# Last layer of a graph network: product order changed, from adj-first in split float32r to weights-first in plain float32, diagonal on VectorE

## What is computed

```
h = relu(layernorm(x))
h = relu(adj @ (h @ Wg0 + bg0)); h = relu(adj @ (h @ Wg1 + bg1))
for p in 1..4:                      # an LSTM over windows of p nodes, its last state
    h[:, p-1::p, :] = lstm_last(Wih[p-1], Whh[p-1], ..., windows of h)
x = x + h
h = relu(layernorm(x))
x = x + diag(adj) @ (h @ W[0]) + triu(adj, 1) @ (h @ W[1]) + tril(adj, -1) @ (h @ W[2]) + bias
```

## Time and profile before

| | |
|---|---|
| median of 3 runs | 424.93 us (424.89 to 425.09) |
| the profiled execution | 424.94 us |
| its span, first to last instruction | 423.2 us |
| granted TensorE clock | 1.00 |
| busy: TensorE / VectorE / ScalarE / GpSimd | 97% / 78% / 66% / 9% |
| first unit of group 1, 2, 3 begins | 110.04, 209.94, 311.48 us |

### The profile page before, as it was taken

One profiled execution on the slowest core, in us unless ns is written; L12 is line 12 of the kernel. 1 busy time (PEld: TensorE's weight loads), 2 busy tenths in 40 slices (PEclk: granted clock), 3 DMA queues, 4 the chain that ended last, 5 costly groups with the idle time before them and its releaser, 6 DMA issues.

```text
span 423.2 us, 7879 instructions
## 1 busy us (share of the span) xinstructions
PE 411.4 (97%) x2628; PEld 368.5 (87%) x2628; DVE 329.7 (78%) x849; ACT 280.8 (66%) x571; POOL 39.2 (9%) x46
## 2 busy tenths in 40 slices
PE   8999999999999999999989999999999999999897
PEld 7787889997878899999868889999887889999787
DVE  5669999989885788797967678878988777767841
ACT  4667766775966576766876576677596676667542
POOL 4910002001100002000200001100110000000300
PEclk9999999999999999999999999999999999999999
DMA  7900000000001000000001000000000000000011
GB/s 229 366 29 2 0 0 2 2 0 2 0 21 38 14 0 15 4 17 2 2 2 38 31 0 12 1 19 0 1 1 19 27 0 14 0 20 2 12 53 62
DMA packets 6081, 11.17 MB, mean 26 GB/s; under 512 B 1056, under 2 KB 4768, under 8 KB 5536
## 3 DMA queue, kind: packets, MB, share of 16 engines
q1 hardware_dynamic: 6048, 10.77, 7.2%
HBM read 6.57 MB, written 4.19 MB: 25 GB/s over the span
## 4 chain that ended last, share of the span: by engine, by line
PE 70%; DVE 19%; ACT 6%; issue 2%; DMA 1%; POOL 1%; SPq 0%; DVEq 0%; ACTq 0%
PE PS L490 9%; PE PS L481 9%; PE PS L482 9%; PE PS L550 9%; PE PS L509 5%; PE PS L533 5%; PE PS L506 5%; PE PS L505 5%; PE PS L430 3%; PE PS L422 3%; ACT GT L750 3%; PE PS L440 3%; PE PS L407 3%; ACT TC L759 2%; DVE CS L874 2%
## 5 line engine op out<-in xcount | busy, mean ns | idle before, releaser
L750 ACT ACTIVATE GT<-PS,BG 128x256 f32<-128x256 f32 (+2 forms) x312 | 158.5, 563 | 48.7 <-PE PS L509 25.9
L481 PE MATMUL PS<-HH,WIH 128*128 128x256 f32 (+2 forms) x312 | 108.3, 348 | 2.3 <-DVE HH L898 1.8
L482 PE MATMUL PS<-HH,WIL 128*128 128x256 f32 (+2 forms) x312 | 102.7, 330 | 0.0
L490 PE MATMUL PS<-HL,WIH 128*128 128x256 f32 (+2 forms) x294 | 97.4, 331 | 0.3
L759 ACT ACTIVATE TC<-CS 128x512 f32<-128x512 f32 (+2 forms) x88 | 45.1, 512 | 47.5 <-DVE CS L874 31.8
L481 PEld LDWEIGHTS PS<-HH,WIH 128*128 128x128 f32 x312 | 59.0, 189 | 7.2 <-DVE HH L898 2.8
L482 PEld LDWEIGHTS PS<-HH,WIL 128*128 128x128 f32 x312 | 59.0, 189 | 3.4
L490 PEld LDWEIGHTS PS<-HL,WIH 128*128 128x128 f32 x294 | 55.5, 189 | 6.0 <-DVE HL L913 1.7
L509 PE MATMUL PS<-SL,WHH 128*128 128x256 f32 (+2 forms) x192 | 60.1, 313 | 0.0
L351 POOL TENSOR_TENSOR RS<-VE,NHALF 128x8 f32<-128x8 f32 (+2 forms) x15 | 26.5, 1766 | 360.8 <-DVE VE L822 360.8
L505 PE MATMUL PS<-SH,WHH 128*128 128x256 f32 (+2 forms) x192 | 59.8, 312 | 0.0
(11 more groups left out here) (91 smaller groups left out, 596.2 us busy)
## 6 DMA issues: line engine op xcount, KB each, us to landing
X<-x_tbd SPq DMA_DIRECT2D x3, 1024.0 KB, 11.6
out_tbd<-X SPq DMA_DIRECT2D x15, 192.0 KB, 1.9
X<-x_tbd SPq DMA_DIRECT2D x4, 256.0 KB, 4.3
WI<-wih_t SPq DMA_DIRECT2D x1, 1024.0 KB, 5.6
out_tbd<-X SPq DMA_DIRECT2D x7, 128.0 KB, 1.7
WH<-whh_t SPq DMA_DIRECT2D x1, 768.0 KB, 7.1
out_tbd<-X SPq DMA_DIRECT2D x1, 256.0 KB, 2.0
WL<-w_l SPq DMA_DIRECT2D x1, 192.0 KB, 7.0
```

The lines of the kernel that those rows point to most:

```text
L481: pe.matmul(dst, WIH[:, p - 1, cols], x_high, start=True, stop=False)
L482: pe.matmul(dst, WIL[:, p - 1, cols], x_high, start=False, stop=False)
L490: mm = pe.matmul(dst, WIH[:, p - 1, cols], x_low, start=False, stop=(j == 0))
L750: act.activation(GT[:, s, q, 0:n], bank(s, q)[:, 0:n], ACT.Tanh if q == C else ACT.Sigmoid, bias=BG[:, 4 * (p - 1) + q:4 * (p - 1) + q + 1 ...
```

## The change

The product is turned round, and works by quads of 4 batches:

- **Centre.** VectorE subtracts the mean from four batches at once (`centre`, 512 columns). It replaces all normalising and splitting; the reciprocal root is applied later.
- **Turn.** Four transposes by TensorE (`last_turn`), then ScalarE's relu of 512 columns into SBUF (`turn_up`).
- **Value.** Per batch one plain float32 matmul of 384 columns against the three weights side by side (`last_value`); ScalarE's copy of it (`copy_value`) applies the reciprocal root and sorts the three parts. The values lie in the raw LSTM weights' buffers.
- **Sum.** Per quad a bias matmul and two plain float32 matmuls of 512 columns, with adj's upper and lower triangle (`last_sum`). The diagonal part is a multiply and add on VectorE (`add_own`), then `add_out` adds the sum.

The tables hold the new pieces with their bank (0 or 1) and what must be read first. `f_after` makes a unit's forget gate wait until the piece on its bank has been read. `early`, `mid` and `late` say where VectorE does its part in a unit: before the cell, after it, or after the low half.

```diff
+START = {(0, 2): (Piece(TURN, 0, 0, None),), (1, 1): (Piece(TURN, 1, 1, None),),
+         (1, 2): (Piece(VALUE, 0, 0, (TURN, 0)),), (2, 0): (Piece(VALUE, 1, 1, (TURN, 1)),),
+         (2, 2): (Piece(VALUE, 2, 0, (VALUE, 0)),), (3, 0): (Piece(VALUE, 3, 1, (VALUE, 1)),),
+         (3, 1): (Piece(VALUE, 4, 0, (VALUE, 2)),), (4, 0): (Piece(SUM, 0, 1, (VALUE, 3)),),
+         (4, 1): (Piece(VALUE, 5, 0, (VALUE, 4)),), (4, 2): (Piece(VALUE, 6, 1, (SUM, 0)),),
+         (5, 0): (Piece(VALUE, 7, 0, (VALUE, 5)),), (5, 1): (Piece(TURN, 2, 1, (VALUE, 6)),),
+         (6, 0): (Piece(VALUE, 8, 1, (TURN, 2)),), (6, 2): (Piece(VALUE, 9, 1, (VALUE, 8)),),
+         (6, 3): (Piece(VALUE, 10, 1, (VALUE, 9)),), (7, 3): (Piece(VALUE, 11, 0, (FORGET, 6)),)}
 STEADY = Plan(
+    at={**START, (5, 2): (Piece(SUM, 1, 0, (VALUE, 7)),),
+        (7, 4): (Piece(SUM, 2, 0, (VALUE, 11)),), (9, 0): (Piece(TURN, 3, 1, (FORGET, 7)),),
+        (10, 3): (Piece(VALUE, 12, 1, (TURN, 3)),), (11, 3): (Piece(VALUE, 13, 0, (FORGET, 10)),),
+        (12, 3): (Piece(VALUE, 14, 1, (FORGET, 11)),), (13, 3): (Piece(VALUE, 15, 0, (FORGET, 12)),),
+        (13, 4): (Piece(SUM, 3, 0, (VALUE, 15)),)},
+    f_after={6: (SUM, 1), 7: (VALUE, 10), 10: (SUM, 2), 11: (VALUE, 12), 12: (VALUE, 13), 13: (VALUE, 14), 16: (SUM, 3)},
+    early={4: ((ADD, 0),), 7: ((OWN, 2),), 13: ((OWN, 3),)},
+    mid={3: ((OWN, 0),)},
+    late={0: ((CENTRE, 2),), 1: ((CENTRE, 3),), 5: ((OWN, 1), (ADD, 1)), 7: ((ADD, 2),), 13: ((ADD, 3),)})
 LATE = Plan(
+    at={**START, (7, 4): (Piece(SUM, 1, 0, (VALUE, 11)),), (13, 4): (Piece(SUM, 2, 0, (FORGET, 12)),)},
+    f_after={6: (VALUE, 7), 7: (VALUE, 10), 10: (SUM, 1), 16: (SUM, 2)},
+    early={4: ((ADD, 0),), 7: ((OWN, 2),)},
+    late={0: ((CENTRE, 2),), 1: ((CENTRE, 3),), 5: ((OWN, 1),), 7: ((ADD, 1),), 13: ((ADD, 2),)})
...
+            def last_turn(g, q, ps):
+                pe.wait_ge(centred, QUADS * g + q + 1)
+                for n in range(PACK):
+                    mm = pe.transpose(as_batches(ps)[:, n, :], H3[:, q * PACK + n, :], IDENT[:, :])
+            def last_value(g, n, ps):
+                pe.matmul(ps[:, 0:PARTS * D], H3T[:, q % 2, b * T:b * T + T],
+                          WL1[:, :, :].rearrange("p k e -> p (k e)"), start=True, stop=True).then_inc(value_mm, 1)
+            def last_sum(g, q, ps):
+                pe.matmul(as_batches(ps), TWO[:, :], BIAS2[:, :].unsqueeze(1).broadcast_to([T, PACK, D]),
+                          start=True, stop=False)
+                pe.wait_ge(value_sb, G * g + q * PACK + PACK)
+                for k in range(SIDES):
+                    mm = pe.matmul(ps, ADJ2[:, k, :], values(q)[:, 1 + k, :], start=False, stop=(k == SIDES - 1))
...
+            def turn_up(g, q, ps):
+                act.activation(H3T[:, q % 2, :], ps, ACT.Relu).then_inc(turn_sb, 1)
+            def copy_value(g, n, ps):
+                act.activation(values(q)[:, 0:PARTS, b * D:b * D + D],
+                               ps[:, 0:PARTS * D].rearrange("p (k e) -> p k e", k=PARTS), ACT.Copy,
+                               scale=RS2[:, n:n + 1]).then_inc(value_sb, 1)
...
+            def centre(g, q):
+                dve.tensor_tensor(H3[:, quad(q), :], X[:, part, :],
+                                  MINUS2[:, quad(q)].unsqueeze(2).broadcast_to([T, PACK, D]),
+                                  ALU.add).then_inc(centred, 1)
+            def add_own(g, q):
+                dve.wait_ge(value_sb, G * g + q * PACK + PACK)
+                dve.scalar_tensor_tensor(out=X[:, part, :], in0=as_batches(values(q)[:, 0, :]), scalar=DIAG[:, 0:1],
+                                         in1=X[:, part, :], op0=ALU.mult, op1=ALU.add).then_inc(own_ready, 1)
+            def add_out(g, q, ps):
+                dve.wait_ge(out_mm, QUADS * g + q + 1)
+                dve.tensor_tensor(X[:, part, :], as_batches(ps), X[:, part, :], ALU.add).then_inc(out_ready, 1)
...
             def next_graph(i):
...
                 bias_y(1, i + 1)
+                centre(i, 0)
+                centre(i, 1)
                 stats2(1, i)
                 low_h(0, i + 1)
```

More of the change, by code:

```diff
@@ L66 @@
 WARM = 16
-ADJP, OUTP = "adj", "out"
+TURN, VALUE, SUM, FORGET = "turn", "value", "sum", "forget"
+Piece = namedtuple("Piece", ["what", "n", "s", "after"])
 Plan = namedtuple("Plan", [
     "at",
[L75 to L79, removed]
+    "f_after",
+    "quads",
+    "early",
+    "mid",
+    "late",
 ])
 FILL = {4: 6, 9: 6, 15: 5}
[L86 to L92, removed]
@@ L106 @@
-CHUNKS = len(STEADY.chunks)
-TAIL = range(LATE.chunks[-1][0], G)
-NORM_AT, SPLIT_AT = 0, 2
+OWN, ADD, CENTRE = "own", "add", "centre"
+START = {(0, 2): (Piece(TURN, 0, 0, None),), (1, 1): (Piece(TURN, 1, 1, None),),
[6 more added lines that the diff above has]
+         (6, 3): (Piece(VALUE, 10, 1, (VALUE, 9)),), (7, 3): (Piece(VALUE, 11, 0, (FORGET, 6)),)}
@@ L117 @@
+LATE_LOW_AT = {7: ("wi",), 9: ("wh",), 18: ("bias",)}
 LATE_ROW_AT = 20
-LATE_ORDER = ("wi", "wh", "adj", "bias")
+LATE_ORDER = ("wi", "wh", "bias")
 CELL_EARLY = (1, 2, 15)
-def chunk_of(plan, n):
-    c = next(c for c, (first, size) in enumerate(plan.chunks) if first <= n < first + size)
-    return c, n == plan.chunks[c][0], n == sum(plan.chunks[c]) - 1
 LN_STATS_AT = {4 + k: range(3 * k, min(3 * k + 3, G)) for k in range(6)}
@@ L320, in _, with store @@
                 sp.dma_start(X[:, g * G:(g + 1) * G, :], x_tbd[:, g * G:(g + 1) * G, :]).then_inc(x_rest, 16)
[L323 to L326, removed]
+            def store(i):
+                for q in range(QUADS):
+                    sp.wait_ge(out_ready, QUADS * i + q + 1)
+                    part = bass.ds(i * G + q * PACK, PACK)
                     sp.dma_start(out_tbd[:, part, :], X[:, part, :]).then_inc(stored, 16)
[L329 to L333, removed]
+            with sp.Fori(0, GROUPS) as i:
+                store(i)
+            sp.wait_ge(stored, 16 * GROUPS * QUADS)
         @block.gpsimd
@@ L381, in _, with group @@
                     done += 1
-            def group(i, more):
+            def group(i, more, used):
                 if more:
@@ L539, in last_out @@
[L539 to L553, removed]
@@ L1062 @@
         "adj_t": a["adj"].T,
+        "adj_diag": np.diagonal(a["adj"]).reshape(T, 1),
         "wg0": a["L0_gnn_Wg0"],
```

334 lines of the change are left out of this document (182 added, 152 removed).

## The result

The changed kernel takes **429.4 us** (median of 4 runs, 428.43 to 429.95), the kernel before, timed beside it, 424.91. The ratio is 1.0103, 95% interval 1.0084 to 1.0122: slower. The forecast was 426.6 with a range of 423.0 to 429.5. So the side held, and the size is short by 2.8 us. And 429.4 lies above the 425.3 to 428.5 of the case that was forecast.

The account below looks back on a forecast made before the run. TensorE, busy 97% of the span, was taken as the bound. The terms -3.8 + 3.0 - 0.4 + 4.1 + 0.3 - 1.3 - 0.3 + 0.1 = +1.7 gave 426.6 us, range 423.0 to 429.5.

Parts of the forecast that it names:

- the case that was forecast: Both waits, between groups and at unit 6's forget gate, bite: 425.3 to 428.5 us, chance 0.42.
- TensorE's work: In each group of 16 batches, 20.0 us removed and 19.0 added on TensorE: -3.8 us in all.
- Centring between groups: Two centrings ahead of low_h leave TensorE idle about 1.0 us at each of three passages: +3.0 us.
- The loop's return: At group 2's start, about 1.0 of TensorE's 1.4 us wait for a late copy stays: -0.4 us.
- Forget gate of unit 6: It waits 2.0 us for VectorE's late read of quad 1's sum, in two STEADY groups: +4.1 us.
- The faster rival: VectorE reads quad 1's sum early enough that unit 6's forget gate does not wait: 422.5 us, chance 0.22.
- Covered waits: TensorE's waits at unit 9 for a gate and a low part are mostly covered by new work: -1.3 us.
- unit 15: The old 0.63 us wait for a copy goes, against a new 0.5 to 1.0: -0.3 us, in LATE.
- the sum of quad 0: Value 6, at unit 4's output gate, waits 0.1 to 0.25 us for VectorE's read: +0.3 over three groups.
- The slower rival: Without fill in units 14 to 17 TensorE waits 1.0 us more in three groups: 429.6 us, chance 0.15.
- The end: After group 3, the first turn fits in; the last sum's copy wait and larger last store cost +0.1 us.
- The clock: Rival: the 64 added transposes drop TensorE's clock to 1.2 GHz, 7.7 us more: 434 us, chance 0.03.

Follow-up runs that it names:

- Experiment 7: Changed kernel with quad 1's sum read early, plus centrings after low_h of stream 0, one before and one after combine2: 422.74 us, ratio 0.9948.
- experiment 3: Changed kernel with the two centrings between groups moved behind low_h of stream 0 and of stream 1, combine2 last: 431.04 us, ratio 1.0142.
- experiment 4: Changed kernel with quad 1's sum read early and the centrings moved behind low_h of stream 0 and of stream 1: 425.29 us, ratio 1.0012.
- experiments 2 and 5: Each on the changed kernel: quad 1's sum read ahead of unit 5's hidden state, 424.37 us; eight dummy matmuls in unit 6's wait, 428.23 us.
- experiment 11: Changed kernel with quad 1's sum read early and the reciprocal root left out of ScalarE's value copy: 423.0 us, one run.

## Why the prediction was right, and where not

- **TensorE's work** (-3.8): right as far as it can be read. The values are 0.64 apart and the sums 0.86, and the units of group 3, where only short waits are new (up to 0.47 by the weight loads), came out 1.1 shorter for 1.3 forecast.
- **Centring between groups** (+3.0): right in place and nearly in size. The idle is 0.74 + 0.30 before unit 0 in group 1, released by low_h, and the same in group 2; in group 3 the 0.81 is put down to ScalarE's high half, which ends just ahead of VectorE's part. To group 1 only 0.4 arrived, because the stretch ahead was 0.4 shorter: VectorE's last bias addition there starts at 106.33, and before at 106.75. So the passage cost some 0.8. Experiment 7 wins back half of it, 1.6 us over three passages.
- **The loop's return** (-0.4): right in kind, and twice as large. By the matmuls 0.57 are left of the 1.38 of the earlier trace rows, by the weight loads 1.01 of 1.81. VectorE's pause is 1.74 here and 1.93 before, and 1.05 in experiment 7; in all three low_h stands last ahead of it. It is 2.83 and 2.95 in experiments 3 and 4, where the short instructions of `combine2` stand last. What the pause consists of no view shows.
- **Forget gate of unit 6** (+4.1): right; the chain is 4.76 for 4.7, and taking the wait away gives 3.9 at an equal clock. The faster rival rested on a shorter chain, and falls.
- **Covered waits, unit 15 and the sum of quad 0** (-1.3, -0.3, +0.3): the stages hold them together within 0.2, but by errors that cancel. The forget gate of unit 9 no longer waits in group 1, the low part still does, 0.32 for 0.36; a value ahead of quad 0's sum waits 0.44, 0.80 and 0.47 by the weight loads in the three groups. Against that the new wait in units 14 to 17 is shorter than the 0.5 to 1.0 that was set against the old one of 0.63. The slower rival, missing fill in those units, has one short row in each group, 0.34 us at 178.95, 0.33 at 281.56 and 0.36 at 376.81 by the weight loads, and falls too. That the time came out near its 429.6 is chance.
- **The end** (+0.1): this step failed; it measured +2.2. It was added up too small to begin with: by its own numbers the wait for the last copy is 0.2 + 0.49 less 0.23, which is 0.46, and the first value comes 0.2 later than the old first product, so 0.6 and not 0.1 even with the store at nothing. Then, three sizes. The last store of 256 KB for 192 KB waits 2.5 us for 1.5, and from the last addition's start to the end it is 1.4 more in all, the largest part. The copy was taken at the 0.49 of the earlier trace rows, a copy without an operand per partition, and is 0.59; TensorE stands idle for it 0.44 before the last sum and, which was not forecast, 0.45 before the old group's last sum. And it stands 0.78 for the turned h3, where the forecast had the turn fit in; the first value starts 0.25 later in the stage than forecast.
- **The clock**: the rival named the wrong cause, and the forecast had no term for the right one. Transposes do not lower it (experiments 2 and 5). The waits that were forecast do, by some 1.7 us for each that is followed by the slow stretch. The run-to-run spread of the changed kernel, 428.25 to 430.26, and most of what its median lies above the profiled 428.43, goes with the mean clock of the runs.

Of the 2.8 us missed, 1.5 stand in the span of the profiled execution (3.2 for 1.7), of which the end makes 2.1 and the first passage gives back 0.6; 0.3 lie outside the span; and about 1.0 is what the median lies above that execution, with the clock.

The 0.10 us of the scale operand is stated in the Trainium skill, "ScalarE: Activation LUTs", What ACT_TABLE_LOAD costs: an operand that is read per partition adds some 93 ns to an ACTIVATE. This case agrees, 591 against 494 ns (experiment 11). It speaks against the 0.49 that the forecast took.

## What to carry to other kernels

Price a wait where it bites, and then ask what the queue behind it does: here a bank read 4.1 us late stopped TensorE twice and cost 5.5 us with the clock, and two VectorE instructions moved half a unit up undid it. Take a duration from a row with the same operands, not only the same shape, and look at the last store by its size. Where an instruction is moved ahead of a loop's end, look at the first wait after it begins anew: the time may only have moved there.

## What was not expected of the hardware

- TensorE stood 1.9 us (2.5 by the weight loads) in a kernel in which it is busy 96% of the span, and 1.4 us of work later its clock was granted at 0.50 for 3.41 us; in experiment 3 a wait of 2.6 us (3.1 by the weight loads) did the same (220.96 to 224.37). It is not sure to follow: of the eight waits of 1.9 to 2.7 us by the matmuls in four profiles (the changed kernel twice, experiments 3 and 4) four were followed by such a stretch: none of two in the changed kernel's first profile, one of two in its second, all three in experiment 3, not the one in experiment 4. What decides it is not shown. In the other profiles the longest wait behind the first 10 us is 1.5 us (in the kernel before), and the clock stayed at 1.00 for as long as TensorE worked.
- A per-partition scale costs ScalarE 0.10 us in a copy of 384 columns; writing three rows of 128 and not one of 384 costs nothing.
- The wait for the last store of 256 KB is 2.3 to 2.8 us over nine profiles; in halves of 128 KB it is 1.6 to 1.7, and at 192 KB, in one profile, it was 1.5.
